# Turning the normalised activations by 16-bit DMA transposes instead of on TensorE (cross-attention and quantised FFN, one core)

## The reference, cut to what matters

```python
x = x + xattn(layernorm(x), ctx, Wq, Wkv)          # softmax over 128 keys
h = layernorm(x)                                   # the h of this document
def act_qdq(x):                                    # one scale for all of x
    scale = max(max(abs(x)) / 32767, 1e-12)
    return clip(round(x / scale), -32768, 32767) * scale
h = act_qdq(h)
up, gate = act_qdq(h @ deq(w_up).T), act_qdq(h @ deq(w_gate).T)    # 512 -> 1536
o = act_qdq(act_qdq(gate * u16(sigmoid(gate))) * up)
return x + o @ deq(w_down).T                       # weights are 4-bit blocks of 32
```

## Time and profile before

| | us |
|---|---|
| median of 3 runs | 913.06 (910.35 to 917.38) |
| the profiled execution, its own time | 914.32 |
| its span, first to last instruction | 912.5 |
| PE busy | 877.3 |
| DVE busy | 658.1 |
| ACT busy | 567.7 |
| POOL busy | 145.8 |

### The profile page before, as it was taken

How to read it: one execution, slowest core, us unless ns; L and a number is a source line. 1 busy time by engine, 2 the same in 40 slices (tenths; PEclk the granted TensorE clock), 3 DMA queues, 4 the chain that set the end, 5 groups by cost and what they waited for, 6 DMA issues and landing times.

```text
span 912.5 us, 12151 instructions
## 1 busy us (share of the span) xinstructions
PE 877.3 (96%) x4308; PEld 442.6 (49%) x4308; DVE 658.1 (72%) x954; ACT 567.7 (62%) x693; POOL 145.8 (16%) x109
## 2 busy tenths in 40 slices
PE   7899979999999999999999989999599989999998
PEld 5788764444444444444444434444344434444443
DVE  4989896732436243279996859855899997999892
ACT  2369977634554354489997858853589975555330
POOL 0189950067001920000000000000000000000000
PEclk9999999999999999999999999999799999999999
DMA  9812226333459649884339994799987787989872
GB/s 342 326 71 117 93 94 242 155 156 138 162 220 294 222 155 294 319 314 162 138 144 334 358 339 145 276 364 354 409 293 264 270 325 273 389 300 394 305 278 106
DMA packets 92319, 226.57 MB, mean 248 GB/s; under 512 B 31984, under 2 KB 31984, under 8 KB 90096
## 3 DMA queue, kind: packets, MB, share of 16 engines
q1 hardware_dynamic: 91120, 221.80, 67.3%
q10 hardware_dynamic: 1152, 4.19, 1.2%
HBM read 127.40 MB, written 92.27 MB: 241 GB/s over the span
## 4 chain that ended last, share of the span: by engine, by line
PE 69%; issue 12%; DMA 8%; DVE 6%; ACT 3%; SPq 2%; POOLq 0%; POOL 0%; DVEq 0%; ACTq 0%
PE ps L837 27%; PE ps L870 16%; PE ps L915 14%; PE ps L942 3%; PE ps L710 3%; PE ps L771 2%; DMA big<-in_L_ffn_w_gate_dram 2%; PE ps L788 2%; DMA up_park<-big 2%; DMA big<-product_park 2%; DMA big<-sign_park 1%; DVE small L1463 1%; PE ps L932 1%; ACT big L960 1%; ACT big L1134 1%
## 5 line engine op out<-in xcount | busy, mean ns | idle before, releaser
L960 ACT ACTIVATE big<-ps 128x1024 f32<-128x1024 f32 (+2 forms) x194 | 153.8, 814 | 192.9 <-PE ps L837 104.5
L870 PE MATMUL ps<-big 128*128 (+1 forms) x1152 | 249.0, 379 | 2.5 <-ACT big L960 2.5
L837 PE MATMUL ps<-big 128*128 (+1 forms) x1152 | 248.8, 379 | 0.2 <-DVE big L1413 0.2
L870 PEld LDWEIGHTS ps<-big 128*128 128x128 f16 x1152 | 112.7, 98 | 138.7 <-issue 3.2
L837 PEld LDWEIGHTS ps<-big 128*128 128x128 f16 x1152 | 112.6, 98 | 136.1 <-DVE big L1413 0.8
L1431 DVE TENSOR_REDUCE small<-big 128x1 f32<-128x1024 f32 (+1 forms) x48 | 58.4, 1219 | 135.9 <-ACT big L960 135.8
L915 PE MATMUL ps<-big 128*128 128x512 f16 x576 | 126.7, 383 | 2.4 <-DVE big L1564 2.4
L915 PEld LDWEIGHTS ps<-big 128*128 128x128 f16 x576 | 56.7, 99 | 71.8 <-issue 5.1
L651 POOL PARTITION_ALL_REDUCE small<-small x9 | 3.6, 404 | 533.5 <-DVE small L1510 181.4
L896 PE MATMUL ps<-big 128*128 128x512 f16 x384 | 85.6, 385 | 3.4 <-ACT big L1167 3.4
L1481 DVE CUSTOM_DVE_ANT_0 big<-big,small 128x1024 f32<-128x1024 int16 x48 | 61.7, 1285 | 7.0 <-DVE small L1475 0.2
(11 more groups left out here) (103 smaller groups left out, 1008.9 us busy)
## 6 DMA issues: line engine op xcount, KB each, us to landing
big<-up_park SPq DMA_DIRECT2D x90, 512.0 KB, 5.7
up_park<-big SPq DMA_DIRECT2D x48, 512.0 KB, 4.8
gate_park<-big SPq DMA_DIRECT2D x42, 512.0 KB, 2.6
big<-gate_park SPq DMA_DIRECT2D x42, 512.0 KB, 6.1
sign_park<-big SPq DMA_DIRECT2D x48, 256.0 KB, 2.2
big<-in_x_dram SPq DMA_DIRECT2D x8, 1024.0 KB, 18.1
x_park<-big SPq DMA_DIRECT2D x8, 1024.0 KB, 3.9
product_park<-big SPq DMA_DIRECT2D x16, 512.0 KB, 6.0
```

Of the source, the lines that this page charges most:

```text
L837: mm = nc.tensor.matmul(ps[:, 2 * (n % 2) + j], w[:, a, k, o:o + P], XT[:, g, b, k], start=(k == 0 and a + b == 0), stop=(k == KC - 1 and ...
L870: mm = nc.tensor.matmul(ps[:, b + j], WU[:, a, k, o:o + P], XT[:, g, c, k], start=(k == 0 and a + c == 0), stop=(k == KC - 1 and c == 1))
L960: return nc.scalar.activation(dst, src, ACT.Copy)
```

## The change

Only group 0 of h (tiles 0 to 3) is still turned on PE (steps 15 to 18) and copied by ACT, into `first_h`. POOL writes all of h in natural layout (tokens on partitions) into `H`, which takes the place of `HT`, with no wait on `ht_mm`. `h_max` reads `H` behind `h2_d`, two tiles at a time (15 reductions of 128x1024), and the last two tiles alone. Behind the scale, ACT writes groups 1 to 7 as natural-layout integers into `hq`; SP issues for each group four DMA transposes of 128x512 16-bit integers into a second pair of buffers, `hx` (`turn_group`); DVE splits `hx`. `h_int(g)` waits until group g-2 has been turned. `turn_group(1)` stands behind the load of the up weights on SP; `turn_group(n+2)` stands between gate store and sign store of unit n. `split_h(n+1)` now stands behind the reduction of unit n, and `split_h(7)` behind all six, ahead of `block_max`.

```diff
 SP:
+            def turn_group(g):
+                sp.wait_ge(hq_d, KC + g)
+                need(sp, hlo_d, KC + g - 2 if g > 2 else 0)
+                turned = hx[:, g % 2].rearrange("p (k i t) -> p k i t", k=KC, i=TI)
+                for i in range(TI):
+                    sp.dma_start(turned[:, :, i], hq[:, g % 2, i * D:(i + 1) * D],
+                                 transpose=True).then_inc((wd_turned, wu_turned)[g % 2], 16)
...
                     sp.dma_start(gate_d[g * UPG + n], gate_out[:, n % 2]).then_inc(g_st[n % 2], 16)
+                    if g == 0 and n + 2 < NG:
+                        turn_group(n + 2)
                     sp.wait_ge(sign_ev, g * UPG + n + 1)
...
+            turn_group(1)
             for g in range(4):
                 park_gate(g)
 POOL:
-                    need(pool, ht_mm, TI * g + i - 3)
-                    nc.gpsimd.tensor_scalar(h2[:, i], X[:, g, i], ...
+                    nc.gpsimd.tensor_scalar(H[:, g, i], X[:, g, i], ...
 PE:
-                if H_LAG <= n < NT + H_LAG:
+                if H_LAG <= n < TI + H_LAG:
                     turn_h(n - H_LAG)
 ACT:
-                if H_LAG < n <= NT + H_LAG:
+                if H_LAG < n <= TI + H_LAG:
                     take_hT(n - H_LAG - 1)
...
             def h_int(g):
-                need(act, hlo_d, g + KC - 2 if g > 1 else 0)
-                nc.scalar.activation(hq[:, g % 2], HT[:, g].rearrange("p k t -> p (k t)"), ACT.Copy,
+                if g == 2:
+                    act.wait_ge(hlo_d, KC)
+                if g > 2:
+                    h_turned(act, g - 2)
+                nc.scalar.activation(hq[:, g % 2], H[:, g].rearrange("p i d -> p (i d)"), ACT.Copy,
                                      scale=col["xinv"]).then_inc(hq_d, 1)
 DVE:
             def h_max(n):
-                dve.wait_ge(ht_ev, n + 1)
-                t = (n % TI) * P
-                nc.vector.tensor_reduce(hcol[:, n:n + 1], HT[:, n // TI, :, t:t + P], AX.XY, ALU.max,
+                lone = n + 2 >= NT
+                if not lone and n % 2 == 0:
+                    return
+                dve.wait_ge(h2_d, n + 1)
+                i, j = n % TI, n - NT // 2 + 1 if lone else n // 2
+                nc.vector.tensor_reduce(hcol[:, j:j + 1], H[:, n // TI, i if lone else i - 1:i + 1], AX.XY, ALU.max,
                                         apply_absolute_value=True).then_inc(hcol_d, 1)
...
             def split_h(g):
-                dve.wait_ge(hq_d, g + KC)
-                nc.vector.tensor_copy(hi, hq[:, g % 2]).then_inc(hhi_d, 1)
+                h_turned(dve, g)
+                nc.vector.tensor_copy(hi, hx[:, g % 2]).then_inc(hhi_d, 1)
                 dve.wait_ge(hhi_d, g + KC)
-                nc.vector.tensor_tensor(lo, hq[:, g % 2], hi, ALU.subtract).then_inc(hlo_d, 1)
-
-            split_h(1)
+                nc.vector.tensor_tensor(lo, hx[:, g % 2], hi, ALU.subtract).then_inc(hlo_d, 1)
+
...
-                    if isinstance(g, int) and g == 0 and n + 2 < NG:
-                        split_h(n + 2)
+                    if isinstance(g, int) and g == 0:
+                        split_h(n + 1)
...
             gate_max(0)
+            split_h(NG - 1)
             linked(block_max(0, 1, wn_ld[1]))
```

More of the change, by code:

```diff
@@ L51 @@
 WTOP = 2048.0
+H_ODD = TI * (NG // 2)
+H_EVEN = TI * (NG // 2 - 1)
 KEPT = 23
@@ L165, in build @@
         HT0 = 16384
-        HT = part(HT0, 16384).rearrange("p (g k t) -> p g k t", g=NG, k=KC)
+        H = part(HT0, 16384).rearrange("p (g i d) -> p g i d", g=NG, i=TI)
         ctx_sb = part(HT0 + 4096, 1024).rearrange("p (b d) -> p b d", b=B)
@@ L195, in build @@
         PTs = part(HT0 + 14336, 1024).bitcast(F16).rearrange("p (s l i t) -> p s l i t", s=2, l=2, i=TI)
-        h2 = part(U0 + 4096, 2048).rearrange("p (s d) -> p s d", s=4)
+        first_h = part(U0 + 4096, 2048).rearrange("p (k t) -> p k t", k=KC)
         hq = part(U0, 2048).bitcast(I16).rearrange("p (s w) -> p s w", s=2)
+        hx = part(U0 + 2048, 2048).bitcast(I16).rearrange("p (s w) -> p s w", s=2)
         shelf = part(HT0, 24576).rearrange("p (j w) -> p j w", j=24)
@@ L276, in build @@
         squares = cut(1248, 256).bitcast(mybir.dt.bfloat16)
-        hcol = cut(1544, 32)
+        hcol = cut(1544, NG * TI // 2 + 1)
         gcol = cut(1544, 48)
@@ L350, in signs_given, with h_turned @@
             return 0 if m < 0 else min(2 * m if m <= 6 else 12 + 3 * (m - 6), NS)
+        def h_turned(eng, g):
+            eng.wait_ge((wd_turned, wu_turned)[g % 2], 16 * TI * ((g + 1) // 2))
         def slot_free(eng, c):
@@ L411, in _ @@
                 park_gate(g)
-            sp.wait_ge(wd_turned, 16 * 2 * KC)
+            sp.wait_ge(wd_turned, 16 * (2 * KC + H_EVEN))
             sp.dma_start(wd_d, wd_prep.rearrange("p l c n -> p (l c n)")).then_inc(wd_st, 16)
@@ L673, in normalise @@
                 for i in range(TI):
-                    need(pool, ht_mm, TI * g + i - 3)
-                    nc.gpsimd.tensor_scalar(h2[:, i], X[:, g, i], negm[:, bass.ds(TI * g + i, 1)],
+                    nc.gpsimd.tensor_scalar(H[:, g, i], X[:, g, i], negm[:, bass.ds(TI * g + i, 1)],
                                             rs2[:, bass.ds(TI * g + i, 1)], ALU.add, ALU.mult).then_inc(h2_d, 1)
@@ L795, in turn_h @@
                 for k in range(KC):
-                    mm = turn(ps[:, 7, k * P:(k + 1) * P], h2[:, n % 4, k * P:(k + 1) * P])
+                    mm = turn(ps[:, 7, k * P:(k + 1) * P], H[:, 0, n, k * P:(k + 1) * P])
                 mm.then_inc(ht_mm, 1)
@@ L861, in _ @@
                 gate(g)
-            pe.wait_ge(wu_turned, 16 * 8)
+            pe.wait_ge(wu_turned, 16 * (2 * KC + H_ODD))
             def raise_unit(g, n):
@@ L1009, in take_hT @@
                 act.wait_ge(ht_mm, n + 1)
-                t = (n % TI) * P
-                copy(HT[:, n // TI, :, t:t + P], ps[:, 7].rearrange("p (k t) -> p k t", k=KC)).then_inc(ht_ev, 1)
+                t = n * P
+                copy(first_h[:, :, t:t + P], ps[:, 7].rearrange("p (k t) -> p k t", k=KC)).then_inc(ht_ev, 1)
             def weights_hi(c, bank):
@@ L1020, in natural_hi @@
                     if m == 2:
-                        act.wait_ge(wu_turned, 16 * 8)
+                        act.wait_ge(wu_turned, 16 * (2 * KC + H_ODD))
                     else:
@@ L1047, in _ @@
             for k in range(KC):
-                nc.scalar.activation(hq[:, 0, k * 512:(k + 1) * 512], HT[:, 0, k], ACT.Copy,
+                nc.scalar.activation(hq[:, 0, k * 512:(k + 1) * 512], first_h[:, k], ACT.Copy,
                                      scale=col["xinv"]).then_inc(hq_d, 1)
             def h_int(g):
-                need(act, hlo_d, g + KC - 2 if g > 1 else 0)
-                nc.scalar.activation(hq[:, g % 2], HT[:, g].rearrange("p k t -> p (k t)"), ACT.Copy,
+                if g == 2:
[3 more added lines that the diff above has]
+                nc.scalar.activation(hq[:, g % 2], H[:, g].rearrange("p i d -> p (i d)"), ACT.Copy,
                                      scale=col["xinv"]).then_inc(hq_d, 1)
@@ L1066, in take_gate @@
                     elif n == 0:
-                        act.wait_ge(wd_turned, 16 * 2 * KC)
+                        act.wait_ge(wd_turned, 16 * (2 * KC + H_EVEN))
                     if not kept and not (isinstance(g, int) and g == 0 and n < 2):
@@ L1340, in natural_lo @@
                 if m == 2 and c == 0:
-                    dve.wait_ge(wu_turned, 16 * 8)
+                    dve.wait_ge(wu_turned, 16 * (2 * KC + H_ODD))
                 nc.vector.tensor_tensor(natural(1, m, c), WN[:, c * D:(c + 1) * D].rearrange("p (k o) -> p k o", k=KC),
@@ L1399, in quant_scale @@
                 return nc.vector.tensor_scalar(col[inv], col[rec], factor, None, ALU.mult)
-            dve.wait_ge(hcol_d, NT)
+            dve.wait_ge(hcol_d, NT // 2 + 1)
             nc.vector.tensor_reduce(col["hmx"], hcol, AX.X, ALU.max).then_inc(col_max, 1)
```

## The result

The changed kernel takes 929.78 us (median of 4 runs, 929.68 to 932.6) beside 914.34 us for the kernel before (4 runs): a ratio of 1.0179, 95% interval 1.0156 to 1.0202. The profiled execution has a span of 928.0 us, 15.5 more than before. 917 with a range of 908 to 927 was forecast; it is 3 us beyond the range, and slower by over 1%, which was given a chance of 0.23.

A forecast was written before the change was run, and what follows sets the result against it. PE was taken to bound the kernel, busy 877 of 912.5 us, with POOL, DVE and ACT close behind in attention. -3.6 (front) + 6.0 (stall) + 1.7 (clock) = +4.1 on 913.1 gave 917.2, stated as 917.0 us; range 908 to 927.

The forecast's parts named there:

- Part 1, the front: Attention stage up to the gate's start: less PE and ACT work, then DVE bounds; gain 3.6 us, bounds 0.7 to 5.
- SP's cost per transpose: SP's queue, groups 1 to 7: issuing one 128x512 transpose takes 0.65 us, 2.6 us a group, less than a unit.
- rival 2: SP's issue bounds the gate stage: 1.48 us per transpose, group 7 landing at 189.6, 14 us stall; 925.2 us, chance 0.18.
- The queue's 2.7 us per group: DMA engines, groups 1 to 7: transposing one 524 KB group takes 2.7 us at 192 GB/s, bounds 1.3 to 5.
- Rival 1: DMA queue without backlog: a group takes at most 2.0 us, stall 1.2 us, no clock loss; 910.7 us, chance 0.27.
- The place that decides: DVE's split of group 7 ahead of the block maximum delays ACT's copy; PE stalls 6.0 us at unit 10.
- slack: At PE's unit 10: 3.3 us between the end of ACT's copy of unit 8 and unit 10's due start.
- the sign of rival 2: Group 7's last transpose landing over 50 us after the gate's start; 42 to 46 would be the forecast.
- The clock: PE behind the stall at unit 10: the granted clock falls to its lower level for four us, 1.7 us lost.
- Cost nothing: Gate's start: a half clock there costs up to 1.7 us, but the stall at unit 10 takes it up.
- 28 fewer PE tiles: Attention stage: 28 tiles of 4 transposes leave PE, 12.2 us of work, of which 3.6 us was to be gained.

The follow-up runs named there:

- the last three kernels: Changed kernel with groups 6 and 7 split late and one transpose per group (18, then 26 dummies), then two transposes and 28 dummies: 913.2, 913.05, 912.03 us.

## Why the prediction was wrong, by its own steps

**Part 1, the front: right.** The `hcol` reduction was forecast at 131.2 and came at 130.86. Its working held less well than its sum: DVE didn't wait for POOL at 117 (the double reduction starts at 117.02 right behind its predecessor, POOL being 1.7 us earlier), and DVE's own work set the end. The gate's first matmul came at 135.29 instead of the forecast 134.4: of the 4.0 us only 2.8 reached the gate, since POOL's maximum over partitions started at 132.40, 1.36 us behind the reduction, with nothing in the profile that it waited for.

**The term that failed: SP's cost per transpose.** The prediction says: "four blocks are between 0.4 and 1.5 us, and I take a third of it with some fixed part, 0.65 us". It is 1.27 us. So the step that SP needs 2.6 us for a group, "less than a unit", failed: it needs 5.4 to 5.6, and with two stores 6.65, more than PE's 5.18. The fixed part is nearly all of an issue: 1.25 us for 2 blocks, 1.27 for 4, none under 1.48 for 8 and for 12 (these with the DMA engines full, so how much of it is back pressure isn't known). The bound had been stated (from 1.2 us on the issue decides) and the range of the cost held it; I picked the value by size where the only row had a single size, and a row of one size says nothing about how a cost divides. With 1.27 us rival 2's own sum gives a cycle of 4 x 1.27 + 0.7 = 5.8 us and a group 7 at about 184; the cycle was 6.65, since the first transpose behind a store cost 1.5 us and the stores 1.0 us together, and the first group was issued at the load's pace, 10.4 us.

**The queue's 2.7 us per group: near.** The kernel with one transpose per group shows a cycle of 4.98 us; less the 1.9 us of stores, an estimate by the plain rate of the earlier trace rows, that is 3.1 us a group. Its stall of 6.5 us stands beside the forecast 6.0. This mechanism was right, but hidden behind SP's. Rival 1 needed 2.0 us a group or less, and the trace says no: 524 KB in 3.1 us are an estimated 169 GB/s beside these stores. The Trainium skill (DMA: Bandwidth & Descriptors, section Latency and other measured facts) gives DMA transposes 261 GB/s, which this trace does not reach.

**The place that decides: right.** The stall is at unit 10, behind DVE's block maximum behind `split_h(7)`. The arithmetic of slack holds too: the block maximum starts 57.2 us after the gate's start instead of 36.1, 21.1 later; less 3.3 of slack that is 17.8, and unit 10 starts 69.7 us after it instead of 51.8, 17.9 later. The gap came over 50 us after the gate's start with group 7 landing at 55, which the prediction had named as the sign of rival 2.

**Rival 2 was the case**, given 0.18 and 925.2 us. The time lies 4.6 us beyond its figure. Of that, 1.2 us is the kernel before, whose median is 914.34 us here and was 913.1 in the sum; 0.8 us is the front, 2.8 instead of 3.6 us at the gate; and 3.8 us is group 7, which lands 55.3 us after the gate's start instead of the 51.5 of rival 2 (189.6 - 138.06), mostly since the first group took 10.4 us at the load's pace and not 5.9. The other way go 0.2 us of the clock behind the gap (1.5 instead of 1.7) and the 1.1 us behind the gate stage.

**The clock: near in size, from a single row.** Behind the 13.0 us it was 0.50 and 0.52 for four us, and 1.5 us were lost there instead of 1.7. At the gate's start the lower level cost PE about 2 us (192 matmuls in 43.58 us, where 8 x 5.18 = 41.4 would do). "Cost nothing" was right for the end all the same: the kernel with only group 7 late kept its clock there, and its units 8 and 9 start no earlier. Where nothing stalls behind it, it is lost, as the profiles with 18 and 26 dummies show. The price came from one gap of 2.41 us, and other gaps didn't keep to it: 2.38 us at unit 10 of the kernel with groups 6 and 7 late cost nothing, and 6.5, 7.0 and 13.6 us in three others cost 2.3, 2.8 and 2.2 us (the 912 matmuls behind them beside 197.01 us).

The range's low end has a slip: 908 lies 2.7 us below rival 1's 910.7, not 1. Nothing hangs on it.

**What of 28 fewer PE tiles came back.** TensorE's transposes fell from 360 to 248, 12 us of PE work as forecast; 4.0 us of it reached the joint, 2.8 the gate, and 1.1 to 1.9 us the end once the queue was relieved (the medians of the last three kernels beside the kernel before), since DVE and POOL had stood within a tenth of PE.

## What to carry to other kernels

Work moved from an engine to the DMA queue has two prices, the issuing engine's time per instruction and the engines' time per byte; work both out against the period of the work beside them, and where only one size is in the trace, take the instruction's price whole as one of the cases. In this kernel one or two large transposes beat four or eight small ones, and a consumer that needs a tile only much later should not wait for it ahead of something urgent. When a stage ends earlier, look at what padded it, here the dummies that kept the clock: they may have to be lengthened by what was saved. Here only the profiles show that gain, 1.7 us, and the runs do not.

## What the runs showed of the hardware that I had not expected

- A 16-bit DMA transpose held SP for 1.25 us at 2 blocks of 128x128 and 1.27 at 4 in the median, and for no less than 1.48 at 8 and 12, where a plain SBUF copy of 128 KB cost 0.6 us and a plain store with a free queue 0.33.
- Between the end of POOL's last tile (126.3) and its maximum over partitions (132.40) lie 6.1 us, though the input is ready at 131.0. It is 5.8 to 6.4 us in all the kernels with the new front, and was 5.7 us before with the input just ready. So a faster DVE alone would most likely not have brought the joint forward in them. What POOL does in that time stays open.
- While the 3 MB load was in flight, the issue of the transposes behind it took its time: 10.4 us for four transposes, 10.3 us for one, 11.4 us where the load was moved ahead of group 2.
- A gap of PE of 2.38 us between two units of the gate left the granted clock at 1.00, where one of 2.41 us in the earlier trace rows was followed by 0.52 and 0.63, and one of 2.16 us at the gate's start by 0.56 and 0.59. The length of a gap alone doesn't say what the clock does behind it.
